# Cross-attention on one core: scores computed transposed in 32x32 tiles of TensorE, blocks turned both ways by VectorE, values in 16 tiles

## The reference

```
q = x @ Wq.T + bq;  k = ctx @ Wk.T + bk;  v = ctx @ Wv.T + bv
scores = (q . k) / sqrt(32), per head;  -1e9 where mask == 0
e = exp(scores - rowmax) * mask;  probs = e / (sum(e) + 1e-9)
y = (probs . v, heads joined) @ Wo.T + bo + x
out = (y - mean(y)) / sqrt(var(y) + 1e-5) * ln_g + ln_b
```

## Time and profile before

| | |
|---|---|
| median of 3 runs | 807.72 us (806.95 to 812.35) |
| span of the profiled execution | 804.6 us |
| what the fastest run shows beyond that span | 2.35 us |
| mean granted clock of TensorE | 0.973 of full speed |
| read from and written to HBM | 23.18 MB and 16.78 MB, 50 GB/s over the span |

### The profile page before, as it was taken

The page is one execution under the profiler, slowest core; times in us unless marked ns, Lnnn a source line. Parts: engine busy times, 40 slices in busy tenths (PEclk is TensorE's granted clock), DMA queues, the critical chain, the costliest instruction groups (busy, mean ns, idle before and its releaser), DMA issues.

```text
span 804.6 us, 13042 instructions
## 1 busy us (share of the span) xinstructions
PE 730.8 (91%) x4289; PEld 576.4 (72%) x4289; DVE 742.5 (92%) x994; ACT 447.9 (56%) x929; POOL 557.9 (69%) x391
## 2 busy tenths in 40 slices
...
DMA packets 23727, 40.87 MB, mean 51 GB/s; under 512 B 4446, under 2 KB 4454, under 8 KB 23655
## 3 DMA queue, kind: packets, MB, share of 16 engines
...
q10 hardware_dynamic: 16, 0.00, 0.0%
HBM read 23.18 MB, written 16.78 MB: 50 GB/s over the span
## 4 chain that ended last, share of the span: by engine, by line
DVE 48%; PE 33%; issue 15%; ACT 2%; DVEq 1%; DMA 1%; POOLq 0%; SPq 0%; POOL 0%
PE bank L347 19%; DVE rowsum L823 7%; DVE E L793 7%; PE bank L494 6%; PE bank L473 6%; DVE Y L879 6%; DVE E L814 4%; DVE bn L865 4%; DVE rowmax L803 4%; DVE xT_AT_lo L774 4%; DVE rowsum_eps L832 3%; DVE Y L857 2%; DVE QT_lo L781 2%; DVE exp_bias L811 2%; DVE inv_sum L841 1%
## 5 line engine op out<-in xcount | busy, mean ns | idle before, releaser
L638 ACT ACTIVATE PT<-bank 77x512 f32<-77x512 f32 x256 | 149.8, 589 | 206.0 <-PE bank L473 206.0
L983 POOL TENSOR_TENSOR E<-E,mask_f 128x1232 f32<-128x1232 f32 x64 | 173.7, 2714 | 117.5 <-ACT E L630 117.4
L993 POOL TENSOR_TENSOR E<-E,inv_sum 128x1232 f32<-128x1232 f32 x64 | 146.2, 2284 | 86.5 <-DVE inv_sum L841 85.2
L473 PEld LDWEIGHTS bank<-ident,E 128*77 128x77 f32 x1024 | 127.3, 151 | 75.2 <-issue 35.0
L473 PE MATMUL bank<-ident,E 128*77 128x128 f32 x1024 | 162.0, 284 | 5.1 <-ACT PT L638 3.5
L793 DVE TENSOR_TENSOR E<-bank,mask_bias 128x616 f32<-128x616 f32 x128 | 98.6, 777 | 15.4 <-PE bank L347 14.3
L972 POOL TENSOR_TENSOR x_bo<-x_in,bo_row 128x512 f32 (+1 forms) x64 | 100.6, 1583 | 14.2 <-DMA bo_row<-in_L_xattn_bo 14.2
L347 PE MATMUL bank<-Kd_hi,QT_lo 128*128 128x308 f32 x256 | 86.9, 340 | 9.9 <-issue 6.0
L879 DVE SCALAR_TENSOR_TENSOR Y<-Y,mean_var,g_row 128x512 f32<-128x512 f32 x64 | 92.0, 1437 | 0.2
L803 DVE TENSOR_REDUCE rowmax<-E 128x16 f32<-128x1232 f32 x64 | 91.0, 1422 | 0.6
L494 PE MATMUL bank<-PT,V_now 77*32 77x512 f32 x512 | 74.5, 661 | 18.4 <-DVE QT_lo L781 16.5
...
## 6 DMA issues: line engine op xcount, KB each, us to landing
...
Y<-in_mask_1x1xSxS_if SPq DMA_DIRECT2D x1, 616.0 KB, 10.5
```

Source lines behind the costliest of these rows:

```text
L473: last = nc.tensor.transpose(pt_bank(s, g)[0:SK, j * P:j * P + P], E[:, (t + 1) % 4, HG * g + j, :], ident[:, :])
L638: cp(PT[0:SK, HG * g:HG * g + HG, i * P:i * P + P], pt_bank(s, g)[0:SK, :].rearrange("p (j r) -> p j r", j=HG), ACT.Copy).then_inc(pt_read ...
L983: nc.gpsimd.tensor_tensor(out=e, in0=e, in1=mask_f[:, bass.ds(b_tile, 1), :] .broadcast_to((P, H, SK)), op=ALU.mult).then_inc(weighted, 1)
L993: nc.gpsimd.tensor_tensor(out=e, in0=e, in1=inv_sum[:, i, :].unsqueeze(2) .broadcast_to((P, H, SK)), op=ALU.mult).then_inc(probs_ready, 1)
```

## The change

The kernel is written anew; the amounts of work in Q and OUT stay. Again there are 16 blocks of 512 rows; all lists are written out without a loop. What it does:

- x arrives twice: turned by the host (`xT`, with the turned weights and a turned mask), and in rows for the residual. `XH` (ScalarE) and `XL` (VectorE) split it, both from SBUF. No `XT` and no Q split: `QE` copies Q once, in full float32.
- `S_round(b, j)`, three of them per block, compute scores transposed: keys in partitions, rows in columns. A round covers 32 of 96 key slots (77 are real). It first writes the mask's bias with 16 matmuls of a 32x32 identity against the mask in bf16, and adds 16 matmuls of 32 head numbers x 32 keys against Q, in 16 different 32x32 tiles, into the four banks of `ring`. Scores come out negated, and a minimum stands for the maximum.
- `TI` (VectorE) turns half a round, 128 x 1024 numbers, in 32x32 blocks from PSUM into `E`: two per round, six per block. A round of scores waits for the two turns of the round before, since there is one ring.
- `MX` takes minima over 78 numbers for 32 (row, head) groups per partition at once, two per block. `EX` (ScalarE) takes exponentials of 77 numbers, 64 per block, each with its own bias and with its sum written out (`accum_out`); they come in 8 groups of 8. `EPS` adds the epsilon, `RC` inverts, `NM` (GpSimd) multiplies, four per block of 128 x 1232 numbers.
- `TO` (VectorE) turns the probabilities back: 128 x 1024 and 128 x 256 numbers, four of each per block, SBUF to SBUF.
- `AV(b, h)` multiplies the values for half the rows in 16 tiles and three rounds of keys, 256 columns each, into the same ring. `AH` and `AL` split the result.
- `OUT` is a product with ones that adds bo, and the twelve matmuls of before. `RS` and `SS` add x and take statistics on VectorE. The rest of the layer norm is on GpSimd: `LN` is three instructions of 128 x 512 per tile, `RD` the inverse root for two tiles at once.

```diff
-                        last = nc.tensor.transpose(pt_bank(s, g)[0:SK, j * P:j * P + P],
-                                                   E[:, (t + 1) % 4, HG * g + j, :], ident[:, :])
-                    last.then_inc(pt_ps, 1)
...
-                def bias(t, half):
...
-                    tt(E[:, t, 2 * HG * half:2 * HG * half + 2 * HG, :].rearrange("p (g j) k -> p g j k", g=2),
-                       scores_ps[:, 2 * half:2 * half + 2, 0:GK].rearrange("p g (j k) -> p g j k", j=HG),
-                       mask_bias[:, bass.ds(bs % BB * T + t, 1), :].unsqueeze(2).broadcast_to((P, 2, HG, SK)),
-                       ALU.add).then_inc(biased, 1)
...
-                    e = E[:, t, 0:HV, :]
-                    tt(e, e, rowmax[:, t, 0:HV].unsqueeze(2).broadcast_to((P, HV, SK)), ALU.subtract) \
-                        .then_inc(shifted, 1)
...
-                def weigh(t):
...
-                    nc.gpsimd.tensor_tensor(out=e, in0=e, in1=mask_f[:, bass.ds(b_tile, 1), :]
-                                            .broadcast_to((P, H, SK)), op=ALU.mult).then_inc(weighted, 1)
...
+            def S_round(b, j):
...
+                if j == 0:
+                    pe.wait_ge(q_ready, 4 * b + 4)
...
+                    if b >= 2:
+                        pe.wait_ge(a_lo, 4 * (b - 2) + 4)
...
+                    pe.wait_ge(turned, 6 * b + 2 * j)
+                for r in range(R):
+                    for c in range(C):
+                        mm(ring[DK * c:DK * c + DK, r, :], ident[DK * r:DK * r + DK, :],
+                           mask_bias[DK * r:DK * r + DK, kb, cols], start=True, stop=False,
+                           tile_position=(DK * r, DK * c))
+                for r in range(R):
+                    for c in range(C):
+                        last = mm(ring[DK * c:DK * c + DK, r, :],
+                                  KT[DK * r:DK * r + DK, c, batch, DK * kb:DK * kb + DK],
+                                  QT[DK * r:DK * r + DK, c, :], start=False, stop=True,
+                                  tile_position=(DK * r, DK * c))
+                last.then_inc(s_ps, 1)
...
+            def AV(b, h):
...
+                pe.wait_ge(back_ready, 4 * b + 2 * h + 2)
+                if h == 0:
+                    pe.wait_ge(turned, 6 * min(b + 2, NB))
+                else:
+                    pe.wait_ge(a_lo, 4 * b + 2)
+                for kb in range(3):
+                    for c in range(C):
+                        for r in range(R):
+                            rows = slice(DK * c, DK * c + DK)
+                            v, p = ((V_main[rows, kb, batch, r, :], PT_main[rows, h, r, :, DK * kb:DK * kb + DK])
+                                    if kb < 2 else (V_tail[rows, batch, r, :], PT_tail[rows, h, r // 2, :, :]))
+                            last = mm(ring[DK * r:DK * r + DK, c, 0:HW], v, p, start=(kb == 0), stop=(kb == 2),
+                                      tile_position=(DK * c, DK * r))
+                last.then_inc(av_ps, 1)
...
+            for m in range(NB + 2):
+                if m > 0:
+                    Q(m, 2), Q(m, 3)
+                OUT(m - 2, 0), AV(m - 2, 1), OUT(m - 2, 1)
+                S_round(m, 0), OUT(m - 2, 2)
+                S_round(m, 1), OUT(m - 2, 3)
+                S_round(m, 2)
+                if m == 0:
+                    K_rest(0), K_rest(1), K_rest(2), K_rest(3), V(0), V(1), V(2), V(3)
+                    pe.wait_ge(v_ready, B)
+                Q(m + 1, 0), Q(m + 1, 1), AV(m - 1, 0)
...
+            def EX(b, h, r):
...
+                for i in range(HQ):
+                    e = E_rows[b % 2][:, r, HQ * h + i, 0:SK]
+                    last = cp(e, e, ACT.Exp, scale=-1.0, bias=rowmin[:, b % 2, h, r, i:i + 1],
+                              accum_out=rowsum[:, b % 2, h, r, i:i + 1])
+                last.then_inc(exp_ready, 1)
...
+            for a in range(-1, NB + 1):
+                if a >= 0:
+                    EX(a, 0, 0), QE(a + 1, 1), EX(a, 0, 1), QE(a + 1, 2), EPS(a, 0, 0)
+                    AH(a - 1, 1)
+                    QE(a + 1, 3), XH(a + 2, 0), EX(a, 0, 2), XH(a + 2, 1), XH(a + 2, 2), XH(a + 2, 3)
+                    EX(a, 0, 3), EX(a, 1, 0), EPS(a, 0, 1), EX(a, 1, 1)
...
+                if a >= 0:
+                    EX(a, 1, 2), EPS(a, 1, 0), EX(a, 1, 3)
+                QE(a + 2, 0)
+                EPS(a, 1, 1), AH(a, 0)
...
+            def TI(b, j, p):
...
+                dve.wait_ge(s_ps, 3 * b + j + 1)
...
+                lo = 2 * p * QH * PITCH + DK * kb
+                dst = E[:, b % 2, lo:lo + 2 * QH * PITCH].rearrange("p (n k) -> p n k", k=PITCH)[:, :, 0:DK]
+                nc.vector.transpose(dst, ring[:, 2 * p:2 * p + 2, :].rearrange("p r (a q) -> p (r a) q", q=DK)) \
+                    .then_inc(turned, 1)
...
+            def MX(b, h):
...
+                nc.vector.tensor_reduce(out=rowmin[:, b % 2, h, :, :],
+                                        in_=E_rows[b % 2][:, :, HQ * h:HQ * h + HQ, 0:SK + 1],
+                                        op=ALU.min, axis=AX.X).then_inc(min_ready, 1)
...
+            def TO(b, h, p):
...
+                dve.wait_ge(probs_ready, 4 * b + 2 * h + p + 1)
+                if b:
+                    dve.wait_ge(av_ps, 2 * (b - 1) + h + 1)
...
+                nc.vector.transpose(PT_main[:, h, 2 * p:2 * p + 2, :, :],
+                                    E_rows[b % 2][:, 2 * p:2 * p + 2, rows, 0:2 * DK])
+                nc.vector.transpose(PT_tail[:, h, p, :, :],
+                                    E_rows[b % 2][:, 2 * p:2 * p + 2, rows, 2 * DK:PITCH]
+                                    .rearrange("p r a k -> p a r k")).then_inc(back_ready, 1)
...
+            def XL(b, k):
+                if not has(b) or b == 0:
+                    return
+                dve.wait_ge(x_hi, 4 * b + k + 1)
+                if k == 0:
+                    dve.wait_ge(q_ps, 4 * b)
+                tt(xT_lo[:, k, :], xT_in[:, k, :], xT_hi[:, k, :].bitcast(FP32), ALU.subtract).then_inc(x_lo, 1)
...
+            for d in range(1, NB + 2):
+                TI(d, 0, 1), TO(d - 1, 0, 0), RS(d - 2, 2), TI(d, 1, 0), SS(d - 2, 2), TI(d, 1, 1)
+                RC(d - 1, 0, 1), RS(d - 2, 3), TI(d, 2, 0), TI(d, 2, 1), XL(d + 1, 0), XL(d + 1, 1)
+                TO(d - 1, 0, 1), XL(d + 1, 2), XL(d + 1, 3), RC(d - 1, 1, 0)
...
+                MX(d, 0), RC(d - 1, 1, 1), SS(d - 2, 3), AL(d - 1, 0), TO(d - 1, 1, 0), TO(d - 1, 1, 1)
+                MX(d, 1), RS(d - 1, 0), RC(d, 0, 0), SS(d - 1, 0), AL(d - 1, 1), RS(d - 1, 1), SS(d - 1, 1)
+                TI(d + 1, 0, 0)
...
+            def NM(b, h, p):
...
+                pool.wait_ge(inv_ready, 4 * b + 2 * h + p + 1)
+                e = E_rows[b % 2][:, 2 * p:2 * p + 2, HQ * h:HQ * h + HQ, 0:SK]
+                tt(e, e, inv_sum[:, b % 2, h, 2 * p:2 * p + 2, :].unsqueeze(3).broadcast_to((P, 2, HQ, SK)),
+                   ALU.mult).then_inc(probs_ready, 1)
...
+            def LN(b, t):
...
+                pool.wait_ge(rstd_ready, 2 * b + t // 2 + 1)
+                nc.gpsimd.tensor_scalar(Y[:, i, :], Y[:, i, :], mean_var[:, i, 0:1], rstd[:, i:i + 1],
+                                        ALU.subtract, ALU.mult).then_inc(centered, 1)
+                pool.wait_ge(centered, n + 1)
+                tt(Y[:, i, :], Y[:, i, :], g_row[:, :], ALU.mult).then_inc(scaled, 1)
+                pool.wait_ge(scaled, n + 1)
+                tt(Y[:, i, :], Y[:, i, :], b_row[:, :], ALU.add).then_inc(normed, 1)
...
+            for g in range(-1, NB + 1):
+                NM(g, 1, 1), RD(g - 1, 1), LN(g - 1, 2), LN(g - 1, 3), NM(g + 1, 0, 0)
+                if g == -1:
+                    wo_low()
+                RD(g, 0), LN(g, 0), NM(g + 1, 0, 1), LN(g, 1), NM(g + 1, 1, 0)
```

1240 lines of the change are left out of this document (452 added, 788 removed).

## The result

The changed kernel takes **768.36 us** (median of 4 runs, 767.64 to 768.83); the kernel before took 807.34 beside it (806.59 to 812.35). The ratio is 0.947, 95% interval [0.941, 0.953]: 39 us faster, where I forecast 99.6. The time is inside the range and the direction is right, but the gain is only two fifths of the forecast. The profiled execution has a span of 765.9 against my 705, so 61 us have to be explained.

A forecast was written before the change was run, and what follows sets the result against it. VectorE bounded the old kernel, TensorE close behind; in the new one the order of waits decides. Start 95, 14 periods of 39.6, last period 28 and tail 28 gave a 705 us span, forecast 708 us, range 648 to 788.

The forecast's parts named there:

- the start: From the beginning to the end of `AV(0, 0)`: 64 us through four groups of `Q`, then 24 and 7 more, 95.
- the period: One block's loop: 36.9 us walked, plus 1.7 for the clock and 1.0 for `XL`, 39.6 us.
- the tail: From the end of `AV(15, 0)` to the end: 28 us, including two layer norms on GpSimd (7.5).
- the packing: TensorE: all 16 tiles run side by side, so a score round takes 1.4 us and a values' half 1.5.
- The sums on ScalarE: ScalarE: each sum written out by an exponential costs 0.10 us, between nothing and 0.203.
- The clock: TensorE: one fall of the granted clock per period after standing still 6.3 us, in `Q`, costing 1.7 us.
- The contention of `XL`: VectorE: four `XL` running while GpSimd works cost between nothing and 3.1 us per period; 1.0 taken.
- GpSimd's bound: GpSimd: each of four `tensor_scalar` per block takes between 0.6 and 1.3 us.
- Row groups in series: Rival on TensorE: the four row groups don't run side by side, 56 us per period, about 975 us; chance 0.06.
- turns at half rate: Rival on VectorE: turns run at half the assumed rate, 48.2 us per period, 833 us; chance 0.05.
- the sums' cost: Rival on ScalarE: sums cost a full 0.203 us each and delay `RC`, 43.7 us per period, 770 us; chance 0.17.
- Rival 1: The walk holds without the clock's fall or `XL` contention, 36.9 us per period, 671 us; chance 0.24.

The follow-up runs named there:

- Experiments 1 and 8: Changed kernel with VectorE's low parts of x ahead of the second round's turns (1: 707.5 us); with both parts of x made a stage earlier (8: 678.5 us).
- experiment 7: Changed kernel with the values' products of 128 columns in place of 256, output wrong: 750.7 us in one execution.
- experiment 3: Changed kernel without the sums that ScalarE's exponentials write out, probabilities not normalised: 766.5 us.
- experiment 2: Changed kernel with 28 idle products on TensorE ahead of its wait for `xT_lo`: 743.5 us.
- experiment 9: Changed kernel with three of the last block's four layer norms done by VectorE and not by GpSimd: 760.0 us.
- Experiment 5: Changed kernel with the loads of block 2's x issued by SyncE before the 24 transfers that place the values: 757.6 us.
- experiment 6: Changed kernel with block 2's x loaded before the values are placed, and also the two parts of Wo made earlier: 754.7 us.

## Why the forecast was right in kind and wrong in size

What failed are four steps of the sum: the start (23 us short), the period (2.5 short in each of 13, 33 in all), the fourteenth period (7 too long) and the tail (10.5 short). The loop that the sum is built on was right.

- **The mechanism: right.** A period set by the order of waits, with no engine full, and TensorE released by `xT_lo`. Experiments 1 and 8 show it: with the same work in another place the kernel is 61 and 90 us faster.
- **VectorE's prices: right.** 1.23, 1.22, 2.70 us for 1.21, 1.21, 2.73.
- **TensorE: the packing held, its price failed.** A score round takes 1.50 (I had 1.4), a values' half 2.05 (1.5). Two halves on the loop are 1.1 us per period, 15 of the 61, the largest term of the period's error. I took 0.07 for a change of tiling, seen at one change between two products; experiment 7 shows 0.79 per half that doesn't go with the columns.
- **The sums on ScalarE: right.** Each leaves a row of its own, 196 ns, but the exponentials start 0.34 apart, 0.09 more than without (I had 0.10 over the earlier trace rows). They are off the loop by experiment 3. My wait of 0.7 ahead of `RC` didn't show, since the turns ahead of it in VectorE's queue, which wait for TensorE, were later than I had them.
- **The clock: right, a little small.** I had 1.7 per period; the trace shows 2.0 in the mean, and experiment 2 gives 1.9 back.
- **The contention of `XL`: right, 1.0.** The two pairs take 1.25 and 2.22. The first pair (from 440.90) stands beside these rows of GpSimd:

```profile
439.40 2.08 POOL L670 TENSOR_SCALAR Y<-Y,mean_var,rstd 128x512 f32<-128x512 f32 x1
441.56 1.72 POOL L673 TENSOR_TENSOR Y<-Y,g_row 128x512 f32<-128x512 f32 x1
```

The first instruction of the pair runs inside the `tensor_scalar` (until 441.48) and isn't slowed; the second pair (from 443.56) runs beside the product and the addition, and is. The Trainium skill ("SBUF — State Buffer", Who interferes with whom) says that a VectorE instruction with two SBUF inputs contends with a GpSimd instruction that reads SBUF, and calls the shared port pair an exclusive lock. If that lock held for the whole of an instruction, the first pair would be late too. The traces disagree for `tensor_scalar`, here and at 753.67 in experiment 9 (0.69, though 0.98 at 752.66), and agree for the products and additions.
- **The rest of the period**, some 1.2 us, is in small pieces that no run takes apart: VectorE's path behind the third round's turns, a little more for each score round and each output product.
- **The start: the step that failed in its mechanism, 23 us.** I wrote "From there to the end of `AV(0, 0)` it is 24 as in the period". I didn't walk SyncE's queue. The 24 transfers that place the values cost it 19.4 us of issuing, 0.66 and 0.88 each, and the loads of block 2's x stand behind them, for which ScalarE waits 10.57. From the end of `Q` to that of `AV(0, 0)` it is 46 and not 31. Experiment 5 gives 10 back with two lines swapped, experiment 6 another 3.6. `TO(0, 0, 0)`, which waits for the last of these transfers until about 81.7 in all these runs, may hold more, which I didn't take apart. The other 8 us stand ahead of that, in the terms up to 64.
- **The tail: the path was wrong, 10.5.** I wrote "two layer norms on GpSimd (7.5)" and put them behind the last statistics. GpSimd's queue sets the end instead: it is full from 726.96 on, with six layer norms in it, of 4.8 each and not 3.7, because `tensor_scalar` takes 2.08. That price alone is 6 to 7 of the 10.5 (an estimate, 6 x 1.1). Experiment 9 gives 7 to 8 back.
- **GpSimd's bound was no bound.** I bounded `tensor_scalar` from above by an addition with more operands. It was slower than that. In the period it changed nothing, since GpSimd waits there; in the tail it did.
- **The rivals.** Row groups in series (975) and turns at half rate (833) are excluded by the profile (a half in 2.05, turns of 1.23), the sums' cost (770) by experiment 3, although that rival gives just the measured time: a time that fits is no evidence for its mechanism. Rival 1 left out both additions, and both came. That 768 is inside my range is luck: the range reached that high for rival 2 and for longer score rounds, and what filled it were the ends and the values' halves.
